# Two residual layers with a masked, per-batch weight on one core: the order of W's and y's work on VectorE and ScalarE

## The chip, the cores and the metric

The kernel runs on one core of a Trainium2 chip. The metric is the time of one execution on the device in microseconds (us), lower is better. The core's engines work side by side, each through its own list of instructions in order, and wait for each other by semaphores: TensorE (PE; PEld is its weight load) multiplies matrices, VectorE (DVE) and ScalarE (ACT) work elementwise, GpSimd (POOL) does little here, and SyncE (SP) issues the DMA transfers.

## The reference

```python
def L0(x, W, b, coeff, mask):
    output = jnp.einsum('bsi,oi->bso', x, W) + b
    sign = (2 * mask - 1).astype(x.dtype)
    diff = jnp.einsum('bsi,bio->bso', x, sign)
    return output + diff * coeff[:, None, None]

def L1(x, adapter_ids, base_weight, base_bias, lora_A_w, lora_B_w):
    result = jnp.einsum('bsd,od->bso', x, base_weight) + base_bias
    A = lora_A_w[adapter_ids]
    Bw = lora_B_w[adapter_ids]
    h = jnp.einsum('bsd,brd->bsr', x, A)
    return result + jnp.einsum('bsr,bor->bso', h, Bw)

x = x + L0(x, L0_cond_W, L0_cond_b, condB_coeff, mask)      # y
x = x + L1(x, ids, base_weight, base_bias, lora_A, lora_B)  # z, the output
```

x is 8 batches x 256 rows x 1024 columns in float32, the mask 8 x 1024 x 1024 in int32, both weights 1024 x 1024. Layer 1's weight is another one in each batch: W + coeff x (2 mask - 1), plus the identity for the residual. Layer 2's weight is the same for all batches, with a low-rank term of rank 16 that goes by the batch's adapter.

## The kernel before

**Parts.** Full float32 accuracy is had from matmuls of a rounded type. Each operand is split in a high part (rounded, ScalarE) and a low part (the rest, VectorE), and three products are summed: high x high, high x low and low x high. So whi and wlo are the parts of W, xhl holds both parts of x, yhl both of y, and w1hi and w1lo those of layer 2's weight.

**Steps.** A step n (0 to 63) is one block of 128 columns of y in one batch: b = n // 8, c = n % 8. TensorE does layer 1 of block n (`layer1(n)`, 16 matmuls, L756 and L758), waits for y's low part of block n-1 (`y_lo`), and then adds block n-1 to the batch's z (`layer2(n - 1, ...)`, 18 matmuls, L800 to L802). z of a batch stands in six PSUM banks until the batch is complete.

- W for a step: `load_mask` brings a block of the mask (512 KB) to one of four slots of wm; `make_w` (VectorE, L589) makes coefficient x mask + W in place; `chunk_hi` (ScalarE, L421) writes the high part, `chunk_lo` (VectorE, L596) the low part. It is made two steps ahead: step n makes W for n + 2.
- y of a step: when layer 1 is complete, `half_y` (ScalarE, L447) takes one half of the bank with the bias to ysum, `make_y` (VectorE, L603) adds the other half, `y_parts_hi` (ScalarE, L454) and `y_parts_lo` (VectorE, L607) write the parts to yhl. Both ysum and yhl have two slots.
- x of the next batch: `turn_rows` (VectorE transpose, L566) in steps c = 3 and 5, `rows_hi` (ScalarE, L432) in the same steps, `rows_lo` (VectorE, L572) in steps c = 4 and 6. The transpose waits for x's four DMAs.
- At a batch's first step (c = 0) TensorE does half of layer 1, then with y's last block the part of layer 2 that holds h, then the other half, and turns h (`turn_h`, L811). ScalarE moves h (`move_h`, L469) and writes its high part (`h_parts_hi`, L476 and L478), VectorE the low part (`h_parts_lo`, L617). Then TensorE ends z with `finish` (L829), and ScalarE and VectorE move three pieces of z each to zst (`move_z`, L489 and L629). TensorE's next layer 2 waits for these moves.

**Order.** The order of each engine's work is written out by hand in loops over n. No scheduler changes it. SyncE's list is in order too. At step n of it stands `load_mask(n + 4)`, which waits for the low part of W of step n; at c = 0 the six stores of z and the six DMAs of bt (`load_bt`) follow, and at c = 1, behind the mask, x of the next batch (`load_x`).

```python
for n in range(NS):
    b, c = divmod(n, KT)
    if n + 4 < NS:
        load_mask(n + 4)
    ...
    if c == 0 and b > 0:
        for q in range(4 if b == 1 else 6):
            store_z(b - 1, q)
        load_bt(b)
    if c == 1 and 0 < b < NB - 1:
        load_x(b + 1)
```

Of the kernel before, what the change touches and what calls it, by code (L numbers as in the profile page):

```python
# [16 lines left out]
def two_layer_kernel(nc, x, coeff, ids, mask, W0, b0, W1, b1, lora_a, lora_b, out):  # L17
    NB, S, D = x.shape
    NL, R, _ = lora_a.shape
    KT = D // P  # L20
    TG = HALF // P
    ST = S // P
    NS = NB * KT
# [37 lines left out]
    def x_split(b, g):  # L61

        return 4 + 2 * (b - 1) + 2 - g
# [5 lines left out]
    def l1_bank(n):  # L69
        if n < KT:  # L70
            return TB[0] if n == 0 else L1B
        return L1B + n % 2
# [12 lines left out]
    def sums_before(b):  # L85

        return 4 + 6 * (b - 1) if b else 0
# [9 lines left out]
    def h_hi_before(b):  # L97
        return 3 + 2 * (b - 1) if b else 0

    with ExitStack() as ctx:  # L100
# [297 lines left out]
        def _(act):  # L398
# [15 lines left out]
            def chunk_hi(n):  # L414
                act.wait_ge(w_made, n + 1)
                if n == 0:
                    act.wait_ge(coeff_made, 2)
                if n >= WS:
                    act.wait_ge(l1_done, n - WS + 1)
                b = n // KT  # L420
                nc.scalar.activation(whi[:, n % WS, :, :], wm[:, n % MS, :].rearrange("p (k o) -> p k o", k=KT),  # L421
                                     ACT.Identity, bias=cs_minus[:, b:b + 1]).then_inc(w_hi, 1)
# [18 lines left out]
            def half_y(n):  # L441
                act.wait_ge(l1_done, n + 1)
                if n == 0:
                    act.wait_ge(b0_moved, 1)
                if n >= 2:
                    act.wait_ge(y_lo, n - 1)
                nc.scalar.activation(ysum[:, n % 2, :], ps[:, l1_bank(n), S:2 * S], ACT.Identity,  # L447
                                     bias=b0col[:, n % KT:n % KT + 1]).then_inc(y_half, 1)

            def y_parts_hi(n):  # L450
                act.wait_ge(y_made, n + 1)
                if n >= 2:
                    act.wait_ge(l2_done, n - 1)
                nc.scalar.activation(yhl[:, n % 2, 0:S], ysum[:, n % 2, :], ACT.Copy).then_inc(y_hi, 1)  # L454

            def first_h_parts_hi():
                act.wait_ge(h_done, 1)
                act.wait_ge(consts_set, 2)
                nc.scalar.activation(ht[0:2 * R, :], ps[0:2 * R, HB, 0:S], ACT.Copy).then_inc(h_hi, 1)
                nc.scalar.activation(ht[64:64 + R, :], ps[0:R, HB, S:2 * S], ACT.Copy).then_inc(h_hi, 1)  # L460
                act.wait_ge(h_hi, 1)
                nc.scalar.activation(ht[96:96 + R, :], ht[0:R, :].bitcast(F32), ACT.Copy).then_inc(h_hi, 1)

            def move_h(b):
                act.wait_ge(h_done, b + 1)
                if b >= 2:
                    act.wait_ge(h_turned, b - 1)
                cut = z_cut(b, 0)[3]
                nc.scalar.activation(h_row[:, :, :], ps[:, ZB[0][0]:ZB[1][0] + 1, cut],  # L469
                                     ACT.Copy).then_inc(h_moved, 1)  # L470

            def h_parts_hi(b):
                act.wait_ge(h_turned, b)
                act.wait_ge(h_cleared, 1)
                act.wait_ge(z_done, sums_before(b))
                nc.scalar.activation(ht[0:R, :], ps[0:R, l1_bank(KT * b + 9), 0:S], ACT.Copy).then_inc(h_hi, 1)  # L476
                act.wait_ge(h_hi, h_hi_before(b) + 1)
                nc.scalar.activation(ht[96:96 + R, :], ht[0:R, :].bitcast(F32), ACT.Copy).then_inc(h_hi, 1)  # L478

            def first_move_z(st):  # L480
                act.wait_ge(z_done, 2 * st + 1)
                nc.scalar.activation(zst[:, st, 0:HALF], ps[:, Z0 + 2 * st, :], ACT.Copy).then_inc(z_moved_act, 1)

            def move_z(b, q):
                st, j = divmod(q, 3)
                act.wait_ge(z_done, sums_before(b) + q + 1)
                act.wait_ge(z_stored[st], 16 * stores_before(b))
                _, cut, cols, _ = z_cut(b, j)
                nc.scalar.activation(zst[:, st, cols], ps[:, ZB[st][j], cut], ACT.Copy).then_inc(z_moved_act, 1)  # L489
# [37 lines left out]
            for n in range(KT, NS):  # L527
                b, c = divmod(n, KT)
                if n == KT:
                    chunk_hi(n + 1)  # L530
                if c == 0 and b >= 2:
                    move_h(b - 1)
                    h_parts_hi(b - 1)
                half_y(n)
                if n == KT:
                    first_h_parts_hi()
                y_parts_hi(n)
                if n == KT:
                    chunk_hi(n + 2)
                    first_move_z(0)  # L540
                    first_move_z(1)
                elif c == 0:
                    for q in (0, 2, 4):
                        move_z(b - 1, q)
                if KT < n < NS - 2:
                    chunk_hi(n + 2)
                if c in (3, 5) and b + 1 < NB:
                    rows_hi(b + 1, 1 - (c - 3) // 2)
            move_h(NB - 1)
# [5 lines left out]
        def _(dve):  # L555
# [13 lines left out]
            def rows_lo(b, g):  # L569
                dve.wait_ge(x_hi, x_split(b, g))  # L570
                k = slice(g * TG, (g + 1) * TG)
                nc.vector.tensor_tensor(xhl[:, b % 2, k, S:2 * S], xt[:, :, :], xhl[:, b % 2, k, 0:S].bitcast(F32),  # L572
                                        ALU.subtract).then_inc(x_lo, 1)
# [9 lines left out]
            def make_w(n):  # L583
                b, c = divmod(n, KT)
                dve.wait_ge(mask_in[n % MS], 16 * (n // MS + 1))
                if b == 0:
                    dve.wait_ge(w0_copied, 2 * (c + 1))
                chunk = wm[:, n % MS, :]
                nc.vector.scalar_tensor_tensor(chunk, chunk.bitcast(I32), cs_twice[:, b:b + 1], w0t[:, c, :, :].rearrange("p k o -> p (k o)"),  # L589
                                               ALU.mult, ALU.add).then_inc(w_made, 1)  # L590

            def chunk_lo(n):
                dve.wait_ge(w_hi, n + 1)
                s = n % WS
                b = n // KT
                nc.vector.scalar_tensor_tensor(wlo[:, s, :, :], wm[:, n % MS, :].rearrange("p (k o) -> p k o", k=KT),  # L596
                                               cs_minus[:, b:b + 1], whi[:, s, :, :].bitcast(F32),
                                               ALU.add, ALU.subtract).then_inc(w_lo, 1)

            def make_y(n):  # L600
                dve.wait_ge(y_half, n + 1)
                row = ysum[:, n % 2, :]
                nc.vector.tensor_tensor(row, ps[:, l1_bank(n), 0:S], row, ALU.add).then_inc(y_made, 1)  # L603
# [6 lines left out]
            def first_h_parts_lo():  # L610
                dve.wait_ge(h_hi, 2)
                nc.vector.tensor_tensor(ht[32:32 + 2 * R, :], ps[0:2 * R, HB, 0:S], ht[0:2 * R, :].bitcast(F32),
                                        ALU.subtract).then_inc(h_lo, 1)

            def h_parts_lo(b):
                dve.wait_ge(h_hi, h_hi_before(b) + 1)
                nc.vector.tensor_tensor(ht[32:32 + R, :], ps[0:R, l1_bank(KT * b + 9), 0:S], ht[0:R, :].bitcast(F32),  # L617
                                        ALU.subtract).then_inc(h_lo, 1)
# [55 lines left out]
            for n in range(KT, NS):  # L674
                b, c = divmod(n, KT)
                if n == KT:
                    chunk_lo(n + 1)
                if c == 0 and b >= 2:
                    h_parts_lo(b - 1)
                make_y(n)  # L680
                if n == KT:
                    first_h_parts_lo()
                if n + 2 < NS:
                    make_w(n + 2)
                y_parts_lo(n)
                if c in (3, 5) and b + 1 < NB:
                    turn_rows(b + 1, 1 - (c - 3) // 2)
                if c in (4, 6) and b + 1 < NB:
                    rows_lo(b + 1, 1 - (c - 4) // 2)
                if n == KT:  # L690
                    first_move_z(0)
                    first_move_z(1)
                elif c == 0:
                    for q in (1, 3, 5):
                        move_z(b - 1, q)
                if n + 2 < NS:
                    chunk_lo(n + 2)
            h_parts_lo(NB - 1)
            for q in (1, 3, 5):
# [242 lines left out]
```

## Time and profile before

| | |
|---|---|
| time, median of 3 runs | 411.49 us (410.44 to 413.1) |
| the profiled execution's own time | 411.09 us |
| its span, first to last instruction | 409.3 us |
| mean granted TensorE clock | 1.00 of full speed |
| TensorE busy | 396.6 us (97%) |
| VectorE busy | 283.1 us (69%) |
| ScalarE busy | 183.8 us (45%) |

The rows further down have start times in us from the start of that span. A timeline row gives the start, the duration, the engine, the line of the program, the operation, and what is written from what. In square brackets stands how long the engine stood idle ahead of it, and what ended that idle time.

### The profile page before, as it was taken

The page shows a single profiled execution, that of the slowest core. Times are in us where ns is not written, and L with a number is a line of the kernel's source. Part 1 is how long each engine was busy: PE and PEld are TensorE (multiplying, and loading weights), DVE is VectorE, ACT ScalarE, POOL GpSimd, SP SyncE. Part 2 cuts the span into 40 slices and gives each one's busy share as a digit, 9 for nine tenths or more (in the row PEclk, how much of TensorE's full clock was granted, in tenths as well). Part 3 has the DMA queues.
Part 4 walks back from the last instruction along what each step waited for, and adds up shares of the span by engine and source line. Part 5 has one row for each costly group of instructions (what it writes and reads, how often), then busy time and mean ns, then how long its engine had stood idle before and what let it go on. Part 6 is the DMA issues. An engine that isn't in the chain of part 4 may idle for free.

```text
span 409.3 us, 6109 instructions
## 1 busy us (share of the span) xinstructions
PE 396.6 (97%) x2358; PEld 364.1 (89%) x2358; DVE 283.1 (69%) x343; ACT 183.8 (45%) x294; POOL 27.4 (7%) x42
## 2 busy tenths in 40 slices
PE   4899999999999999999999999999999999999995
PEld 3787788899999999999999999999999999999994
DVE  1667978867876688577886679575986679575622
ACT  3565675543444344344444345353444334353322
POOL 2224121000001000010001000010001000000000
PEclk9999999999999999999999999999999999999999
DMA  8999986259531893159531893249731793246002
GB/s 282 267 284 270 272 220 172 73 151 254 150 102 57 200 246 98 58 141 246 166 103 56 200 217 110 75 129 216 200 98 49 197 232 107 88 130 168 0 2 103
DMA packets 93633, 63.33 MB, mean 155 GB/s; under 512 B 3612, under 2 KB 90916, under 8 KB 93605
## 3 DMA queue, kind: packets, MB, share of 16 engines
q1 hardware_dynamic: 93586, 62.95, 58.3%
q8 instruction: 19, 0.31, 0.3%
q14 instruction: 10, 0.07, 0.1%
q10 hardware_dynamic: 18, 0.00, 0.0%
HBM read 51.39 MB, written 8.39 MB: 146 GB/s over the span
## 4 chain that ended last, share of the span: by engine, by line
PE 95%; DMA 2%; SPq 1%; DVE 1%; issue 0%; POOL 0%; ACT 0%; DVEq 0%
PE ps L756 29%; PE ps L758 15%; PE ps L802 13%; PE ps L801 13%; PE ps L800 13%; PE ps L734 4%; DMA w0raw<-in_L_cond_W_dram 2%; PE ps L780 2%; PE ps L778 2%; PE ps L779 2%; PE ps L829 2%; PE ps L766 1%; PE ps L811 0%; DVE wm L589 0%; POOL w0raw L341 0%
## 5 line engine op out<-in xcount | busy, mean ns | idle before, releaser
L756 PE MATMUL ps<-xhl,whi 128*128 128x512 f32 x512 | 184.8, 399 | 0.0
L758 PE MATMUL ps<-xhl,wlo 128*128 128x256 f32 x512 | 143.4, 280 | 0.0
L756 PEld LDWEIGHTS ps<-xhl,whi 128*128 128x128 f32 x512 | 96.5, 188 | 20.0 <-DVE xhl L579 0.4
L800 PE MATMUL ps<-w1hi,yhl 128*128 128x344 f32 (+1 forms) x336 | 108.1, 322 | 0.0
L802 PE MATMUL ps<-w1hi,yhl 128*128 128x344 f32 (+1 forms) x336 | 107.7, 321 | 0.0
L801 PE MATMUL ps<-w1lo,yhl 128*128 128x344 f32 (+1 forms) x336 | 107.6, 320 | 0.0
L596 DVE SCALAR_TENSOR_TENSOR wlo<-wm,cs_minus,whi 128x1024 fp32r<-128x1024 f32 x64 | 81.6, 1274 | 25.3 <-ACT whi L421 25.2
L758 PEld LDWEIGHTS ps<-xhl,wlo 128*128 128x128 f32 x512 | 97.0, 189 | 0.3
L421 ACT ACTIVATE whi<-wm,cs_minus 128x1024 fp32r<-128x1024 f32 x64 | 73.7, 1152 | 43.0 <-DVE wm L589 42.9
L589 DVE SCALAR_TENSOR_TENSOR wm<-wm,cs_twice,w0t 128x1024 f32<-128x1024 int32 x64 | 83.8, 1310 | 10.3 <-ACT w0t L402 8.4
L447 ACT ACTIVATE ysum<-ps,b0col 128x256 f32<-128x256 f32 x64 | 30.3, 474 | 85.5 <-PE ps L758 85.3
L800 PEld LDWEIGHTS ps<-w1hi,yhl 128*128 128x128 f32 x336 | 63.1, 188 | 2.6
L603 DVE TENSOR_TENSOR ysum<-ps,ysum 128x256 f32<-128x256 f32 x64 | 27.1, 424 | 53.1 <-ACT ysum L447 53.1
L801 PEld LDWEIGHTS ps<-w1lo,yhl 128*128 128x128 f32 x336 | 63.2, 188 | 0.0
L802 PEld LDWEIGHTS ps<-w1hi,yhl 128*128 128x128 f32 x336 | 63.1, 188 | 0.0
L454 ACT ACTIVATE yhl<-ysum 128x256 fp32r<-128x256 f32 x64 | 26.7, 417 | 28.6 <-DVE ysum L603 27.5
L566 DVE STREAM_TRANSPOSE xt<-xraw 128x1024 f32<-128x1024 f32 x14 | 31.1, 2220 | 4.2 <-DMA xraw<-in_x_dram 4.2
L607 DVE TENSOR_TENSOR yhl<-ysum,yhl 128x256 fp32r<-128x256 f32 x64 | 27.5, 430 | 1.5 <-ACT yhl L454 1.5
L432 ACT ACTIVATE xhl<-xt 128x1024 fp32r<-128x1024 f32 x14 | 14.9, 1061 | 20.5 <-DVE xt L566 20.5
L356 POOL CAST w1hi<-at 128x128 fp32r<-128x128 f32 x7 | 6.6, 940 | 223.7 <-PE ps L802 223.7
L572 DVE TENSOR_TENSOR xhl<-xt,xhl 128x1024 fp32r<-128x1024 f32 x14 | 17.1, 1221 | 0.2 <-ACT xhl L432 0.2
L734 PE MATMUL ps<-ident,w0raw 128*128 128x128 f32 x64 | 11.3, 313 | 5.7 <-POOL w0raw L341 5.7
(68 smaller groups left out, 217.3 us busy)
## 6 DMA issues: line engine op xcount, KB each, us to landing
wm<-in_mask_Bx4096x_ik_dram SPq DMA_DIRECT2D x64, 512.0 KB, 4.4
xraw<-in_x_dram SPq DMA_DIRECT2D x28, 256.0 KB, 5.8
w0raw<-in_L_cond_W_dram SPq DMA_DIRECT2D x8, 512.0 KB, 7.2
w1raw<-_L_cond_base_weight_dram SPq DMA_DIRECT2D x8, 512.0 KB, 7.4
out_dram<-zst SPq DMA_DIRECT2D x20, 172.0 KB, 2.1
bt<-bhl SPq DMA_DIRECT2D x48, 64.0 KB, 2.3
out_dram<-zst SPq DMA_DIRECT2D x8, 176.0 KB, 2.2
out_dram<-zst SPq DMA_DIRECT2D x8, 164.0 KB, 2.2
```

The source lines that it names most:

```text
L421: nc.scalar.activation(whi[:, n % WS, :, :], wm[:, n % MS, :].rearrange("p (k o) -> p k o", k=KT), ACT.Identity, bias=cs_minus[:, b:b + 1] ...
L447: nc.scalar.activation(ysum[:, n % 2, :], ps[:, l1_bank(n), S:2 * S], ACT.Identity, bias=b0col[:, n % KT:n % KT + 1]).then_inc(y_half, 1)
L566: nc.vector.transpose(xt[:, :, :].rearrange("p t (n q) -> p n t q", q=Q), xraw[:, :, :].rearrange("p n (i k) -> p n k i", k=KT)[:, :, g * ...
L589: nc.vector.scalar_tensor_tensor(chunk, chunk.bitcast(I32), cs_twice[:, b:b + 1], w0t[:, c, :, :].rearrange("p k o -> p (k o)"), ALU.mult, ...
L596: nc.vector.scalar_tensor_tensor(wlo[:, s, :, :], wm[:, n % MS, :].rearrange("p (k o) -> p k o", k=KT), cs_minus[:, b:b + 1], whi[:, s, :, ...
L607: nc.vector.tensor_tensor(yhl[:, n % 2, S:2 * S], ysum[:, n % 2, :], yhl[:, n % 2, 0:S].bitcast(F32), ALU.subtract).then_inc(y_lo, 1)
L734: op = nc.tensor.transpose(ps[:, bank, m * P:(m + 1) * P], cut[m], ident[:, :])
L756: nc.tensor.matmul(ps[:, bank, :], whi[:, s, k, :], xhl[:, b % 2, k, :], start=(k == 0), stop=False, skip_group_check=True)
L758: op = nc.tensor.matmul(ps[:, bank, 0:S], wlo[:, s, k, :], xhl[:, b % 2, k, 0:S], start=False, stop=(k == KT - 1), skip_group_check=True)
L800: nc.tensor.matmul(dst, hi, w1hi[:, c, cols], start=(c == 0), stop=False, skip_group_check=True)
L801: nc.tensor.matmul(dst, hi, w1lo[:, c, cols], start=False, stop=False, skip_group_check=True)
L802: op = nc.tensor.matmul(dst, lo, w1hi[:, c, cols], start=False, stop=(c == KT - 1), skip_group_check=True)
```

## The change

In the loop over steps 8 to 63, from step 9 on, VectorE's and ScalarE's work for W of step n + 2 is put ahead of the work for y of step n. Before, VectorE's order was sum of y, product of W, low part of y, transpose or low part of x, moves of z, low part of W. Now it is product of W, low part of x, low part of W, sum of y, low part of y, transpose of x, moves of z. ScalarE's high part of W goes from the end of the step to ahead of the half of y. Step 8 and the steps of batch 0 keep their order. No instruction is added or taken away, and TensorE's, GpSimd's and SyncE's lists stay as they are.

```diff
@@ -531,6 +531,8 @@
                 if c == 0 and b >= 2:
                     move_h(b - 1)
                     h_parts_hi(b - 1)
+                if KT < n < NS - 2:
+                    chunk_hi(n + 2)
                 half_y(n)
                 if n == KT:
                     first_h_parts_hi()
@@ -542,8 +544,6 @@
                 elif c == 0:
                     for q in (0, 2, 4):
                         move_z(b - 1, q)
-                if KT < n < NS - 2:
-                    chunk_hi(n + 2)
                 if c in (3, 5) and b + 1 < NB:
                     rows_hi(b + 1, 1 - (c - 3) // 2)
             move_h(NB - 1)
@@ -677,23 +677,26 @@
                     chunk_lo(n + 1)
                 if c == 0 and b >= 2:
                     h_parts_lo(b - 1)
+                if KT < n < NS - 2:
+                    make_w(n + 2)
+                if c in (4, 6) and b + 1 < NB:
+                    rows_lo(b + 1, 1 - (c - 4) // 2)
+                if KT < n < NS - 2:
+                    chunk_lo(n + 2)
                 make_y(n)
                 if n == KT:
                     first_h_parts_lo()
-                if n + 2 < NS:
                     make_w(n + 2)
                 y_parts_lo(n)
                 if c in (3, 5) and b + 1 < NB:
                     turn_rows(b + 1, 1 - (c - 3) // 2)
-                if c in (4, 6) and b + 1 < NB:
-                    rows_lo(b + 1, 1 - (c - 4) // 2)
                 if n == KT:
                     first_move_z(0)
                     first_move_z(1)
                 elif c == 0:
                     for q in (1, 3, 5):
                         move_z(b - 1, q)
-                if n + 2 < NS:
+                if n == KT:
                     chunk_lo(n + 2)
             h_parts_lo(NB - 1)
             for q in (1, 3, 5):
```

VectorE at a batch's first step (c = 0), before. In brackets stand the semaphores that an instruction waits for: h_hi and y_hi are ScalarE's high parts, y_half its half of y, w_hi its high part of W, mask_in a mask's landing.

```order
L617 TENSOR_TENSOR ht<-ps,ht 16x256 [waits h_hi]
L603 TENSOR_TENSOR ysum<-ps,ysum 128x256 [waits y_half]
L589 SCALAR_TENSOR_TENSOR wm<-wm,cs_twice,w0t 128x1024 [waits mask_in2]
L607 TENSOR_TENSOR yhl<-ysum,yhl 128x256 [waits y_hi]
L629 COPY zst<-ps 128x344 [waits z_stored0,z_done]
L629 COPY zst<-ps 128x336 [waits z_stored1,z_done]
L629 COPY zst<-ps 128x344 [waits z_stored1,z_done]
L596 SCALAR_TENSOR_TENSOR wlo<-wm,cs_minus,whi 128x1024 [waits w_hi]
```

The same step of VectorE in the changed kernel:

```order
L617 TENSOR_TENSOR ht<-ps,ht 16x256 [waits h_hi]
L589 SCALAR_TENSOR_TENSOR wm<-wm,cs_twice,w0t 128x1024 [waits mask_in2]
L596 SCALAR_TENSOR_TENSOR wlo<-wm,cs_minus,whi 128x1024 [waits w_hi]
L603 TENSOR_TENSOR ysum<-ps,ysum 128x256 [waits y_half]
L607 TENSOR_TENSOR yhl<-ysum,yhl 128x256 [waits y_hi]
L629 COPY zst<-ps 128x344 [waits z_stored0,z_done]
L629 COPY zst<-ps 128x336 [waits z_stored1,z_done]
L629 COPY zst<-ps 128x344 [waits z_stored1,z_done]
```

The sum of y (L603) and with it the moves of z (L629) now stand behind both of VectorE's instructions for W.

ScalarE at the same step, before. l1_done is TensorE's end of a layer 1, l2_done that of a layer 2, w_made VectorE's product.

```order
L469 ACTIVATE h_row<-ps 128x32 [waits h_turned,h_done]
L476 ACTIVATE ht<-ps 16x256 [waits z_done,h_cleared,h_turned]
L478 ACTIVATE ht<-ht 16x256 [waits h_hi]
L447 ACTIVATE ysum<-ps,b0col 128x256 [waits y_lo,l1_done]
L454 ACTIVATE yhl<-ysum 128x256 [waits l2_done,y_made]
L489 ACTIVATE zst<-ps 128x328 [waits z_stored0,z_done]
L489 ACTIVATE zst<-ps 128x352 [waits z_stored0,z_done]
L489 ACTIVATE zst<-ps 128x344 [waits z_stored1,z_done]
L421 ACTIVATE whi<-wm,cs_minus 128x1024 [waits l1_done,w_made]
```

The same step of ScalarE in the changed kernel:

```order
L469 ACTIVATE h_row<-ps 128x32 [waits h_turned,h_done]
L476 ACTIVATE ht<-ps 16x256 [waits z_done,h_cleared,h_turned]
L478 ACTIVATE ht<-ht 16x256 [waits h_hi]
L421 ACTIVATE whi<-wm,cs_minus 128x1024 [waits l1_done,w_made]
L447 ACTIVATE ysum<-ps,b0col 128x256 [waits y_lo,l1_done]
L454 ACTIVATE yhl<-ysum 128x256 [waits l2_done,y_made]
L489 ACTIVATE zst<-ps 128x328 [waits z_stored0,z_done]
L489 ACTIVATE zst<-ps 128x352 [waits z_stored0,z_done]
L489 ACTIVATE zst<-ps 128x344 [waits z_stored1,z_done]
```

The high part of W (L421) has gone from behind the moves of z to ahead of the half of y (L447).

## Rows read from the trace of the kernel before

**Rows 1.** The page's busy time: us, share of the span, instructions.

```profile
PE 396.6 (97%) x2358; PEld 364.1 (89%) x2358; DVE 283.1 (69%) x343; ACT 183.8 (45%) x294; POOL 27.4 (7%) x42
```

**Rows 2.** The page's chain of waits that ended last, by engine.

```profile
PE 95%; DMA 2%; SPq 1%; DVE 1%; issue 0%; POOL 0%; ACT 0%; DVEq 0%
```

**Rows 3.** Timeline of TensorE, first matmuls of layer 2 in steps 32 to 34.

```profile
216.48 0.32 PE L800 MATMUL ps<-w1hi,yhl 128*128 128x344 f32 x1
...
224.71 0.33 PE L800 MATMUL ps<-w1hi,yhl 128*128 128x352 f32 x1
...
230.37 0.32 PE L800 MATMUL ps<-w1hi,yhl 128*128 128x352 f32 x1
```

**Rows 4.** Waits between 120 and 400 us: total us, times, longest.

```profile
DVE ysum L603 <- ACT ysum L447: 46.8, 49, 4.3
```

**Rows 5.** Timeline of VectorE in steps 31 and 32.

```profile
213.29 1.28 DVE L589 SCALAR_TENSOR_TENSOR wm<-wm,cs_twice,w0t 128x1024 f32<-128x1024 int32 x1
214.48 0.42 DVE L607 TENSOR_TENSOR yhl<-ysum,yhl 128x256 fp32r<-128x256 f32 x1
215.78 1.28 DVE L596 SCALAR_TENSOR_TENSOR wlo<-wm,cs_minus,whi 128x1024 fp32r<-128x1024 f32 x1 [0.88 <-ACT whi L421]
219.66 0.41 DVE L617 TENSOR_TENSOR ht<-ps,ht 16x256 fp32r<-16x256 f32 x1 [2.60 <-ACT ht L476]
220.61 0.42 DVE L603 TENSOR_TENSOR ysum<-ps,ysum 128x256 f32<-128x256 f32 x1 [0.54 <-ACT ysum L447]
...
222.58 1.34 DVE L629 COPY zst<-ps 128x344 f32<-128x344 f32 x3
```

**Rows 6.** Timeline of ScalarE in steps 31, 32 and 35.

```profile
214.60 1.15 ACT L421 ACTIVATE whi<-wm,cs_minus 128x1024 fp32r<-128x1024 f32 x1 [0.77 <-DVE wm L589]
...
221.07 0.42 ACT L454 ACTIVATE yhl<-ysum 128x256 fp32r<-128x256 f32 x1 [0.49 <-DVE ysum L603]
...
242.09 1.07 ACT L432 ACTIVATE xhl<-xt 128x1024 fp32r<-128x1024 f32 x1 [2.60 <-DVE xt L566]
```

**Rows 7.** Timeline of VectorE, low part of h in batches 2 and 6.

```profile
127.07 0.41 DVE L617 TENSOR_TENSOR ht<-ps,ht 16x256 fp32r<-16x256 f32 x1 [2.60 <-ACT ht L476]
...
312.27 0.41 DVE L617 TENSOR_TENSOR ht<-ps,ht 16x256 fp32r<-16x256 f32 x1 [2.60 <-ACT ht L476]
```

**Rows 8.** Timeline of VectorE, x's first transposes in batches 2 to 6; one low part.

```profile
146.44 2.22 DVE L566 STREAM_TRANSPOSE xt<-xraw 128x1024 f32<-128x1024 f32 x1 [0.40 <-DMA xraw<-in_x_dram]
...
192.32 2.25 DVE L566 STREAM_TRANSPOSE xt<-xraw 128x1024 f32<-128x1024 f32 x1
...
239.88 2.18 DVE L566 STREAM_TRANSPOSE xt<-xraw 128x1024 f32<-128x1024 f32 x1 [1.23 <-DMA xraw<-in_x_dram]
...
245.42 1.22 DVE L572 TENSOR_TENSOR xhl<-xt,xhl 128x1024 fp32r<-128x1024 f32 x1
...
285.83 2.21 DVE L566 STREAM_TRANSPOSE xt<-xraw 128x1024 f32<-128x1024 f32 x1 [0.85 <-DMA xraw<-in_x_dram]
...
332.48 2.18 DVE L566 STREAM_TRANSPOSE xt<-xraw 128x1024 f32<-128x1024 f32 x1 [1.23 <-DMA xraw<-in_x_dram]
```

**Rows 9.** Timeline of TensorE in the first layer 1.

```profile
16.00 0.63 PE L756 MATMUL ps<-xhl,whi 128*128 128x512 f32 x1
...
16.64 0.58 PE L756 MATMUL ps<-xhl,whi 128*128 128x512 f32 x1
...
17.74 0.50 PE L756 MATMUL ps<-xhl,whi 128*128 128x512 f32 x1
18.08 0.28 PE L758 MATMUL ps<-xhl,wlo 128*128 128x256 f32 x1
18.20 0.40 PE L756 MATMUL ps<-xhl,whi 128*128 128x512 f32 x1
```

**Rows 10.** Timeline of the SyncE queue, batch 3's z and the next mask.

```profile
221.85 3.60 SPq L286 DMA_DIRECT2D out_dram<-zst  x6
...
229.30 0.60 SPq L224 DMA_DIRECT2D wm<-in_mask_Bx4096x_ik_dram  x1
```

**Rows 11.** The page's DMA issues: KB each, median us from issue to landing.

```profile
wm<-in_mask_Bx4096x_ik_dram SPq DMA_DIRECT2D x64, 512.0 KB, 4.4
```

## The prediction

> **What bounds the kernel now.** I read the page's busy shares first, then its chain of waits, then the timelines of TensorE, VectorE and ScalarE around one batch boundary. TensorE is busy 97% of the span and VectorE 69% [rows 1]; the chain that ends last lies on TensorE for 95% [rows 2]. Past start-up TensorE hardly waits. One step of it, layer 1 of output block n and then layer 2 of block n-1, takes 230.37 - 224.71 = 5.66 us [rows 3]. So nothing that VectorE or ScalarE do faster can shorten the middle of the span, and the question is only whether the new order makes them late.
>
> They are not busy all the time because they wait: between 120 and 400 us VectorE stands 46.8 us in 49 waits for ScalarE's half of y [rows 4], which itself waits for the end of layer 1. The change puts W's work for step n+2 into that gap. Whether it fits is a matter of one serial chain, not of busy shares.
>
> **The new chain of one step.** The order of work of the new kernel is, on VectorE: product (L589), low part (L596), sum of y (L603), low part of y (L607). On ScalarE: high part of W (L421), half of y (L447), high part of y (L454). Each of the six other than the half of y now waits for the one before it on the other engine, since VectorE's low part of W follows ScalarE's high part, and the sum of y is queued behind that low part. Durations: product 1.28, low part of W 1.28, sum of y 0.42, low part of y 0.42 [rows 5]; high part of W 1.15, high part of y 0.42 [rows 6]. A hand-over between the two engines costs 0.03 to 0.04 (product ends 214.57, high part starts 214.60; that ends 215.75, low part starts 215.78; sum ends 221.03, high part of y starts 221.07) and the next instruction on the same engine starts about 0.08 before the end of the one ahead (214.48 against 214.57) [rows 5, 6]. So from a product to the next product:
> 1.28 + 0.03 + 1.15 + 0.03 + 1.28 - 0.08 + 0.42 + 0.04 + 0.42 + 0.04 + 0.42 - 0.08 = 4.95 us.
> That is less than 5.66, so a step without other work is made up with 0.7 us to spare. In the old order the product lay beside ScalarE's high part of y and ScalarE's high part of W beside VectorE's other work, which is why the old order had more room at equal busy time.
>
> **The rest of a batch.** Eight steps of TensorE take 46.30 us ((312.27 - 127.07) / 4, the low part of h in batches 2 and 6 [rows 7]). I follow batch 4 from that low part at 219.66 [rows 5], since VectorE waits there for TensorE in either order: it starts free of what went before.
> - low part of h: 0.41 - 0.08 = 0.33
> - eight chains, for y of blocks 32 to 39: 8 x 4.95 = 39.6
> - three moves of z, after y of block 32: 1.34 - 0.08 = 1.26 [rows 5]
> - two transposes of x, after y of 35 and of 37: 2.18 - 0.08 and 2.23 - 0.08, about 4.25 (2.18 to 2.25 long [rows 8])
> - x's high parts on ScalarE (1.07 [rows 6]) lie beside VectorE's product of 1.28, and x's low parts (1.22 [rows 8]) beside ScalarE's high part of W with its two hand-overs, 1.15 + 0.03 + 0.03 = 1.21: nothing; at worst 0.1 each
> - the overlap at the end, since the last value must be complete: 0.08
> The sum is 45.5 us to the end of the low part of y of block 39. TensorE wants that value in the middle of layer 1 of block 40, and starts 0.04 later with some 0.10 for the restart (the first matmul after a wait at the start of the kernel took 0.50, a usual one 0.40 [rows 9]). From there to the next low part of h are 219.66 - 216.48 = 3.18 us [rows 3, 5]. Batch: 45.5 + 0.14 + 3.18 = 48.8 us against 46.30, so **2.5 us more in each batch** without any wait for data. The steps on the way: y of block 32 ends 5.4 us after 219.66, at 225.0, and TensorE wants it at 224.71 [rows 3]; y of 33 ends 231.2 against 230.37, so the first waits come at once.
>
> **Wait for x.** The move of z now comes behind W's work. ScalarE's high part of y of block 32 started at 221.07; now it starts at 219.66 + 0.33 + 1.28 + 0.03 + 1.15 + 0.03 + 1.28 - 0.08 + 0.42 + 0.04 = 224.14, 3.07 later. The SyncE queue is in order: the stores of z wait for these moves (221.85 [rows 10]), behind them stand bt's rows, then a mask (229.30) and then x of the next batch. All of it shifts by 3.07. The transpose of x waited for x already in four of batches 2 to 6 (those at 146.44, 239.88, 285.83 and 332.48; the one at 192.32 just did not) [rows 8]. New landing: old + 3.07. VectorE is free for it 0.33 + 4 x 4.95 + 1.26 = 21.4 us after the low part of h, in batch 4 at 241.05; x is there at 242.95. Waits by batch, with the low parts of h 46.30 apart: 1.0, 0.6, 1.9, 1.5, 1.8, together 6.8 us. These go straight into the chain. The mask ahead of x is wanted at 236.1 and lands at 229.30 + 3.07 + 4.4 = 236.8 [rows 10, 11]; what VectorE loses there it would have waited for x anyway.
>
> **The ends.** Batch 7 loads no x; its second y comes 0.33 + 4.95 + 1.26 + 4.95 + 0.08 + 0.14 = 11.7 us after the low part of h, TensorE wants it after 230.37 - 219.66 = 10.7: 1.0 us, and nothing after that. Batch 1 keeps the old order at its first step and waits for no moves: between 0 and 2.5 - 1.26 = 1.2; I take 0.7. The last two steps have no W in either order.
>
> **Sum.** 5 x 2.5 + 6.8 + 1.0 + 0.7 = 21.0 us. The profiled execution took 411.09 with a span of 409.3, which lies 0.4 below the median of 411.49; so 430.3 for the new span, 432.1 for such an execution and 432.5 against the median. The product, made 4.7 us earlier relative to layer 1, gains nothing: no wait of TensorE for W is in the middle of the span to be removed.
>
> **Rivals.** (1) *No loss.* The chains would have to overlap more than I believe: TensorE's waits vanish if a chain takes 4.95 - 2.5/8 = 4.6 us and x lands as before. Every term has a row, so only the shift of x can be softer. If x lands early enough for all batches, 21.0 - 6.8 = 14.2 are left: 425.7. For no measurable change both must hold; that would give 411 to 415. Chance 0.06. (2) *Faster.* A W that is ready a step earlier would take away waits of TensorE for W's low part and let the mask's slot come free sooner. For it speaks that 46.8 us of VectorE's idle time is filled. Against it: TensorE is covered to 95% by its own work [rows 2]; the mechanism decides only if those gaps of TensorE that the rows do not show are waits for W. All that is outside TensorE in the chain is 5% and start-up has nearly all of it; a hundredth of the span, 4 to 5 us, is the most: 407. Chance 0.02. (3) *The clock.* The granted clock is at its full level over the whole span on the page, and a matmul after TensorE's wait at 17.74 took 0.50; the two before it began 0.64 apart with 0.63 and 0.58 for one, against 0.40 later [rows 9], which could be a lower clock that the page does not show. The new kernel makes four or five waits per batch, one of up to 2 us. If after the longest in each batch one step ran at 1.2 GHz in place of 2.4, it would take some 5.66 us more, of which 0.7 is room: 5 x 5 = 25 on top, 457. The start speaks for it only after much longer gaps. Chance 0.05.
> The Trainium skill ("TensorE: Matmul & The Clock Gate", section "A second HAM failure mode: psum-queue depth-cycling") says that short, frequent idle spells between groups of matmuls can make the clock swing between its two levels. By that rule rival 3 would hold; the trace before has no such spells past start-up to test it.
> (4) *More wait for data.* x and three masks share the queue; every further us of x's landing costs 5 us. Part of the range.
>
> **Numbers.** Forecast 0.87, rivals 0.06, 0.02, 0.05. A chain is known to about 0.05 us, which is 40 x 0.05 = 2 us; x may land 1.5 us earlier or 1 us later than I have it, which is -6.1 (the five waits cut to 0, 0, 0.4, 0 and 0.3) to +5 us. That gives 424 to 440. Changes under 1% (4 us) are about what a measurement of this kernel cannot tell from none. Faster 0.02, same 0.06, slower 0.92.
>
> **What would show it.** The chain of waits goes from TensorE over to VectorE and ScalarE, with product, high part, low part, sum, high, low of y in turn. Low parts of h lie 49 to 51 us apart, not 46.3. TensorE's load at L800 waits for L607 four to five times per batch, longest for block 36. The transpose of x waits 1 to 2 us for its DMA. If TensorE's step stays at 5.66 everywhere and h keeps its spacing, the chain is wrong; if the spacing is 48.8, x is.

## The result and the profile after

The changed kernel takes 432.53 us (median of 4 runs, 430.74 to 433.2), the kernel before 412.1 us in the runs beside it. The ratio is 1.0499 with a 95% interval of 1.0459 to 1.0538: 5% slower. The profiled execution took 433.2 us, its span is 431.4 us against 409.3.

The page's busy time and its chain of waits, after:

```profile
PE 404.4 (94%) x2358; PEld 363.9 (84%) x2358; DVE 285.8 (66%) x343; ACT 179.5 (42%) x294; POOL 22.3 (5%) x42
PE 36%; DVE 31%; ACT 13%; SPq 8%; DMA 7%; issue 3%; POOL 1%; DVEq 0%
```

VectorE and ScalarE are busy for nearly as many us as before (285.8 against 283.1, 179.5 against 183.8 [rows 1]) and for a smaller share of the span. What changed is the chain: TensorE holds 36% of it, not 95% [rows 2]. VectorE and ScalarE are far from full, yet the kernel is slower, and the chain names who sets the pace.

The waits between 120 and 420 us (total, times, longest), after:

```profile
ACT whi L421 <- DVE wm L589: 69.0, 37, 4.1
ACT yhl L454 <- DVE ysum L603: 62.6, 48, 1.3
DVE wlo L596 <- ACT whi L421: 45.1, 37, 1.2
DVE yhl L607 <- ACT yhl L454: 23.2, 48, 0.5
PE ps L803 <- DVE yhl L607: 13.5, 28, 1.2
DVE wm L589 <- DMA wm<-in_mask_Bx4096x_ik_dram: 6.7, 4, 2.3
DVE ysum L603 <- ACT ysum L447: 3.6, 1, 3.6
```

The wait that the change wanted to fill, VectorE's for the half of y, is gone but for the last two steps, which have no W (46.8 us before [rows 4]; the one of 3.6 us here and one of 4.3 us at 420.30). In its place VectorE and ScalarE wait for each other, and TensorE has a new wait: 28 times at the first matmul of layer 2 (L803 here) for y's low part. It waits nowhere else in this stretch. The 13.5 us are only its idle time; what a wait costs beyond that stands further down.

VectorE's timeline in batch 4 after, which answers to [rows 5]:

```profile
227.99 0.41 DVE L617 TENSOR_TENSOR ht<-ps,ht 16x256 fp32r<-16x256 f32 x1 [3.35 <-ACT ht L476]
228.43 1.28 DVE L589 SCALAR_TENSOR_TENSOR wm<-wm,cs_twice,w0t 128x1024 f32<-128x1024 int32 x1
230.94 1.28 DVE L596 SCALAR_TENSOR_TENSOR wlo<-wm,cs_minus,whi 128x1024 fp32r<-128x1024 f32 x1 [1.22 <-ACT whi L421]
232.14 0.41 DVE L603 TENSOR_TENSOR ysum<-ps,ysum 128x256 f32<-128x256 f32 x1
233.04 0.43 DVE L607 TENSOR_TENSOR yhl<-ysum,yhl 128x256 fp32r<-128x256 f32 x1 [0.48 <-ACT yhl L454]
233.38 1.35 DVE L629 COPY zst<-ps 128x344 f32<-128x344 f32 x3
234.64 1.28 DVE L589 SCALAR_TENSOR_TENSOR wm<-wm,cs_twice,w0t 128x1024 f32<-128x1024 int32 x1
...
239.59 1.28 DVE L589 SCALAR_TENSOR_TENSOR wm<-wm,cs_twice,w0t 128x1024 f32<-128x1024 int32 x1
...
246.91 1.28 DVE L589 SCALAR_TENSOR_TENSOR wm<-wm,cs_twice,w0t 128x1024 f32<-128x1024 int32 x1 [2.30 <-DMA wm<-in_mask_Bx4096x_ik_dram]
...
251.86 2.19 DVE L566 STREAM_TRANSPOSE xt<-xraw 128x1024 f32<-128x1024 f32 x1
...
279.25 0.41 DVE L617 TENSOR_TENSOR ht<-ps,ht 16x256 fp32r<-16x256 f32 x1 [3.35 <-ACT ht L476]
```

Up to 239.59 each row waits for ScalarE or follows at once: the serial chain. From product to product (234.64 to 239.59) it is 4.95 us. The batch is 279.25 - 227.99 = 51.26 us long, against 46.3 [rows 7]. In it lies one wait for data, 2.30 us, and it is for the mask. The transpose of x shows no wait, unlike [rows 8].

The SyncE queue in that batch, after, against [rows 10]:

```profile
233.36 2.91 SPq L286 DMA_DIRECT2D out_dram<-zst  x6
236.31 3.13 SPq L276 DMA_DIRECT2D bt<-bhl  x5
239.49 0.59 SPq L277 DMA_DIRECT2D bt<-bhl  x1
240.12 0.60 SPq L224 DMA_DIRECT2D wm<-in_mask_Bx4096x_ik_dram  x1
```

The first store begins 233.36 - 227.99 = 5.4 us after the low part of h (2.2 before), the mask is issued 12.1 us after it (9.6 before) and lands 6.8 us later, at 246.91. VectorE was ready for it at 244.6.

TensorE around the wait of that step:

```profile
250.95 0.28 PE L761 MATMUL ps<-xhl,wlo 128*128 128x256 f32 x1
252.00 0.43 PE L803 MATMUL ps<-w1hi,yhl 128*128 128x352 f32 x1 [0.77 <-DVE yhl L607]
252.26 0.32 PE L804 MATMUL ps<-w1lo,yhl 128*128 128x352 f32 x1
```

The first matmul after a wait takes 0.43 and the next one 0.32, as in a stretch without waits. But the wait costs more than its 0.77 us of idle time. From the last matmul of layer 1 to the second of layer 2 are 252.26 - 250.95 = 1.31 us here and 224.87 - 224.59 = 0.28 before, as the timeline of the kernel before shows:

```profile
224.59 0.28 PE L758 MATMUL ps<-xhl,wlo 128*128 128x256 f32 x1
224.71 0.33 PE L800 MATMUL ps<-w1hi,yhl 128*128 128x352 f32 x1
224.87 0.32 PE L801 MATMUL ps<-w1lo,yhl 128*128 128x352 f32 x1
```

That is 1.03 us later, 0.26 more than the idle time. In a dense stretch the matmuls overlap in the trace (each starts before the end of the one ahead), so part of the loss counts as busy: TensorE is busy 404.4 us in place of 396.6 for the same 2358 matmuls. The 28 waits by this reading cost 13.5 + 28 x 0.26 = 20.8 us, an estimate from this wait (two others of the batch, at 233.52 and 259.01, have 0.27 for the 0.26), near the 22.1 us that the span grew.

### The profile page after: what moved, and what is told of

Same layout as the page of the kernel before. It is cut to its first block, busy times and chain, and to the rows that moved or that the text cites. A ratio compares the mean times of both kernels' runs of the same rounds, so it can differ in the third digit from the quotient of the medians.

```text
span 431.4 us, 6109 instructions
## 1 busy us (share of the span) xinstructions
PE 404.4 (94%) x2358; PEld 363.9 (84%) x2358; DVE 285.8 (66%) x343; ACT 179.5 (42%) x294; POOL 22.3 (5%) x42
## 4 chain that ended last, share of the span: by engine, by line
PE 36%; DVE 31%; ACT 13%; SPq 8%; DMA 7%; issue 3%; POOL 1%; DVEq 0%
PE ps L759 10%; DVE wlo L596 10%; DVE wm L589 10%; ACT whi L421 9%; DVE xt L566 5%; PE ps L761 5%; PE ps L803 4%; PE ps L737 4%; DMA wm<-in_mask_Bx4096x_ik_dram 4%; PE ps L805 4%; PE ps L804 4%; ACT yhl L454 3%; SPq L276 3%; DVE ysum L603 3%; SPq L286 2%
## 5 line engine op out<-in xcount | busy, mean ns | idle before, releaser
L803 PE MATMUL ps<-w1hi,yhl 128*128 128x344 f32 (+1 forms) x336 | 111.3, 331 | 13.5 <-DVE yhl L607 13.5
L421 ACT ACTIVATE whi<-wm,cs_minus 128x1024 fp32r<-128x1024 f32 x64 | 73.7, 1151 | 82.8 <-DVE wm L589 81.3
L805 PE MATMUL ps<-w1hi,yhl 128*128 128x344 f32 (+1 forms) x336 | 107.7, 321 | 0.0
L589 DVE SCALAR_TENSOR_TENSOR wm<-wm,cs_twice,w0t 128x1024 f32<-128x1024 int32 x64 | 83.1, 1299 | 16.4 <-ACT w0t L402 8.7
L803 PEld LDWEIGHTS ps<-w1hi,yhl 128*128 128x128 f32 x336 | 63.1, 188 | 24.2 <-DVE yhl L607 22.9
L447 ACT ACTIVATE ysum<-ps,b0col 128x256 f32<-128x256 f32 x64 | 29.3, 458 | 16.1 <-PE ps L761 16.1
L603 DVE TENSOR_TENSOR ysum<-ps,ysum 128x256 f32<-128x256 f32 x64 | 26.7, 418 | 8.3 <-ACT ysum L447 8.3
L617 DVE TENSOR_TENSOR ht<-ps,ht 16x256 fp32r<-16x256 f32 x7 | 2.9, 414 | 23.6 <-ACT ht L476 23.6
```

What stands on the lines that cost most here:

```text
L803: nc.tensor.matmul(dst, hi, w1hi[:, c, cols], start=(c == 0), stop=False, skip_group_check=True)
L805: op = nc.tensor.matmul(dst, lo, w1hi[:, c, cols], start=False, stop=(c == KT - 1), skip_group_check=True)
```

## The experiments

In what follows a *chain* is one step's serial chain, from one product of W to the next. The theory: from batch 1 on, the length of a batch is the serial sum of VectorE's and ScalarE's hand-overs, 8 chains with z's moves and x's transposes, plus what VectorE waits for data that the late moves of z push back. TensorE only follows. The rivals: a *fixed lateness* (each us of W's work ahead of y costs in proportion), and *the queue* (all of the loss comes from z's late moves and what stands behind the stores). All times are medians, all ratios are to the kernel before (411.7 to 411.9 us beside these runs). Where two altered kernels are compared, the difference of their medians is given; taken from the ratios it comes out 1 to 2.5 us smaller or larger, so it is no closer than that.

**One part alone: the product first.** Of the kernel before, in VectorE's list:

```diff
+                if KT < n < NS - 2:
+                    make_w(n + 2)
                 make_y(n)
                 if n == KT:
                     first_h_parts_lo()
-                if n + 2 < NS:
                     make_w(n + 2)
```

> The kernel before with one part of the change alone: VectorE's product of W goes ahead of the sum of y; both parts of W stay behind y. Theory of the serial chain (the batch's length is the sum of the hand-overs between VectorE and ScalarE): the product lies beside ScalarE's half of y, and behind it come sum, high part of y, then ScalarE's high part of W and VectorE's low part: 1.20 + 0.42 + 0.04 + 0.42 - 0.10 + 1.15 + 0.03 + 1.20 = 4.36 us per step, well below the 5.66 of TensorE; a batch by that chain is 44.4 us, under 46.3. So 412, as the kernel before, within 1%. Rival of a fixed lateness (any W work ahead of y keeps TensorE waiting in proportion to its time): the product is 1.28 of the 3.7 us put ahead of y, a third of the 20 us, so 419. Rival of the queue (all comes from z's moves being late): they are late by about 0.7 of 3.1 us, 416.

Measured: 411.88 us, ratio 1.0008 (0.9986 to 1.003). No loss, as the chain says, and fixed lateness and queue are both out at their numbers: z's first store was late as the queue rival has it (in batch 4 it began 2.9 us after the low part of h in place of 2.2), and nothing was lost by it. The waits of this run (120 to 420 us) show a second thing:

```profile
DVE xt L566 <- DMA xraw<-in_x_dram: 9.8, 5, 2.9
DVE wm L589 <- DMA wm<-in_mask_Bx4096x_ik_dram: 3.5, 4, 1.3
```

VectorE waits here for 13.3 us for data, twice as long as in the changed kernel, and it costs nothing, since VectorE has room in the old order of the parts. The same kind of wait costs its full length where VectorE's chain sets the pace.

**Half undone: the low part of W behind y.** Of the changed kernel, in VectorE's list:

```diff
                     rows_lo(b + 1, 1 - (c - 4) // 2)
-                if KT < n < NS - 2:
-                    chunk_lo(n + 2)
                 make_y(n)
...
-                if n == KT:
+                if n + 2 < NS:
                     chunk_lo(n + 2)
```

> The changed kernel with VectorE's low part of W put back behind y; product and ScalarE's high part of W stay ahead. Serial chain: ScalarE's half of y is now queued behind the high part and nothing of VectorE lies beside it: 1.28 + 0.03 + 1.15 - 0.10 + 0.46 + 0.04 + 0.42 + 0.04 + 0.42 + 0.04 + 0.42 - 0.08 + 1.28 - 0.08 = 5.32 us per step in place of 4.95. Seven of them and the 4.20 of the last up to the low part of y make the batch 1.8 us longer than in the changed kernel without waits for data; the mask is wanted 1.1 later and comes 0.8 earlier, so most of its wait (1.35 on average) goes. Together 0.7 us more per batch: 434 to 438, slower than the changed kernel although y comes earlier in each step's list. Rival of fixed lateness: y has 2.4 in place of 3.7 us ahead of it: about 425. Rival of the queue: z's moves are late by 2.2 in place of 3.1: about 426.

Measured: 437.56 us, ratio 1.0652 (1.062 to 1.0684). Slower than the changed kernel although less stands ahead of y. This is where the theories differ most, and only the serial chain has the sign and the size. VectorE's timeline in this run:

```profile
242.57 1.28 DVE L589 SCALAR_TENSOR_TENSOR wm<-wm,cs_twice,w0t 128x1024 f32<-128x1024 int32 x1
245.43 0.42 DVE L603 TENSOR_TENSOR ysum<-ps,ysum 128x256 f32<-128x256 f32 x1 [1.58 <-ACT ysum L447]
246.34 0.42 DVE L607 TENSOR_TENSOR yhl<-ysum,yhl 128x256 fp32r<-128x256 f32 x1 [0.48 <-ACT yhl L454]
246.68 1.28 DVE L596 SCALAR_TENSOR_TENSOR wlo<-wm,cs_minus,whi 128x1024 fp32r<-128x1024 f32 x1
247.88 1.28 DVE L589 SCALAR_TENSOR_TENSOR wm<-wm,cs_twice,w0t 128x1024 f32<-128x1024 int32 x1
```

The chain is 247.88 - 242.57 = 5.31 us (5.32 expected): VectorE stands 1.58 us while ScalarE does the high part of W and then the half of y. TensorE waits in this run for W's low part too, but only once at a matmul, 0.4 us; by the waits that is no second cause of this size.

**The old order at the batch's first step.** In the changed kernel both engines do step c = 0 as before:

```diff
-                if KT < n < NS - 2:
+                if KT < n < NS - 2 and c > 0:
                     chunk_hi(n + 2)
...
-                if KT < n < NS - 2:
+                if KT < n < NS - 2 and c > 0:
                     make_w(n + 2)
...
-                if KT < n < NS - 2:
+                if KT < n < NS - 2 and c > 0:
                     chunk_lo(n + 2)
                 make_y(n)
                 if n == KT:
                     first_h_parts_lo()
+                if c == 0:
                     make_w(n + 2)
```

and the high and the low part of W behind z's moves at c = 0.

> The changed kernel with the old order in each batch's first step (c = 0) alone, on both engines. Serial chain: y of that step is out after 2.9 us and z is moved as early as before, so the mask and x are issued as in the kernel before; from the low part of h to the next step's product 5.4 us in place of 6.65. Then seven chains of 4.95: 5.38 + 34.65 + 0.08 + 4.25 + 0.14 + 3.18 = 47.7 us a batch against 46.3, next to no wait for the mask. 5 x 1.4 + 0.7 in batch 1, nothing in batch 7: 8 us over the kernel before, 420. Queue rival: all gone, 412. Fixed lateness: seven of eight steps are left, 429.

Measured: 419.46 us, ratio 1.0203 (1.0159 to 1.0248). ScalarE's first high part of h in batches 2 and 7 of this run:

```profile
128.72 0.38 ACT L476 ACTIVATE ht<-ps 16x256 fp32r<-16x256 f32 x1 [1.43 <-PE ps L816]
...
367.22 0.38 ACT L476 ACTIVATE ht<-ps 16x256 fp32r<-16x256 f32 x1 [1.43 <-PE ps L816]
```

(367.22 - 128.72) / 5 = 47.70 us a batch, the expected 47.7. One step of eight done in the old order takes away 13 of 20 us (12 by the ratios): the chain loses 1.3 us there and the mask comes in time (0.3 us of waits for it are left).

**The mask and x ahead of the stores.** SyncE's list of the changed kernel:

```diff
-                if n + 4 < NS:
+                if n + 4 < NS and not (c == 1 and b > 0):
                     load_mask(n + 4)
...
                 if c == 0 and b > 0:
+                    load_mask(n + 5)
+                    if b < NB - 1:
+                        load_x(b + 1)
                     for q in range(4 if b == 1 else 6):
                         store_z(b - 1, q)
                     load_bt(b)
-                if c == 1 and 0 < b < NB - 1:
-                    load_x(b + 1)
```

> The changed kernel with SyncE's list altered: at a batch's first step the next mask and x's four loads are issued ahead of the stores of z and bt's rows. Nothing else. Serial chain: the waits of VectorE for the mask (2.0, 0, 2.3, 1.2, 1.2 in the changed kernel's trace) go, low parts of h lie 48.9 to 49.1 us apart in each batch, 5 x 2.7 + 1.0 + 0.8 = 15 us over the kernel before: 426 to 427. Queue rival: 412, since mask and x are early now. Fixed lateness: 427 too.

Measured: 426.7 us, ratio 1.0402 (1.0354 to 1.0449). No wait of VectorE for DMA is left between 120 and 420 us. The page's chain of waits of this run:

```profile
DVE 39%; PE 36%; ACT 16%; DMA 4%; issue 2%; SPq 1%; POOL 0%; DVEq 0%
```

VectorE has more of the chain than TensorE. ScalarE's timeline, first high part of h in batches 2 and 7:

```profile
126.47 0.38 ACT L477 ACTIVATE ht<-ps 16x256 fp32r<-16x256 f32 x1 [1.43 <-PE ps L815]
...
371.06 0.38 ACT L477 ACTIVATE ht<-ps 16x256 fp32r<-16x256 f32 x1 [1.43 <-PE ps L815]
```

A batch is (371.06 - 126.47) / 5 = 48.92 us. By the medians 5.8 of the 20.4 us lost are waits for data that the queue held back; by the ratios 4.0, by the length of the five batches in the two traces 7.1 (251.7 against 244.6 us). So 4 to 7 us go with early data, and 13 to 16 us stay.

**A shorter chain.** The run before, with half of each product left out from step 11 on, so that the output is not the reference's:

```diff
+                h = slice(0, D // 2 if n > KT + 2 else D)
-                nc.vector.scalar_tensor_tensor(chunk, chunk.bitcast(I32), cs_twice[:, b:b + 1], w0t[:, c, :, :].rearrange("p k o -> p (k o)"),
+                nc.vector.scalar_tensor_tensor(chunk[:, h], chunk[:, h].bitcast(I32), cs_twice[:, b:b + 1],
+                                               w0t[:, c, :, :].rearrange("p k o -> p (k o)")[:, h],
                                                ALU.mult, ALU.add).then_inc(w_made, 1)
```

> The run with the hoisted mask and x, and the product of W made over only 512 of its 1024 columns from step 11 on (the other half of W stays the bare mask in its raw form: part of the computation is left out). The order of work is the changed kernel's. Serial chain: the product takes about 0.7 in place of 1.28, a chain 4.37, a batch 48.9 - 8 x 0.58 = 44.3 us, less than TensorE's 46.3: TensorE binds again, 412 to 414. Fixed lateness: y is still 3.1 of 3.7 us late, 412 + 15 x 3.1 / 3.7 = 425.

Measured: 412.11 us, ratio 0.999 (0.9963 to 1.0016). All of the loss is gone with the order of the changed kernel kept. The groups by line and shape of this run show the product's length (busy us, mean ns). Below it stands the page's chain of waits:

```profile
L591 DVE SCALAR_TENSOR_TENSOR wm<-wm,cs_twice,w0t 128x512 f32<-128x512 int32 x53 | 39.1, 738 | 0.2
```

```profile
PE 90%; DMA 5%; SPq 2%; POOL 1%; issue 1%; DVE 0%; DVEq 0%
```

0.54 us less per chain, 4.3 per batch: by the sum 48.9 - 4.3 = 44.6, under TensorE's 46.3, and TensorE has the chain again.

**A longer chain, in both orders.** One more instruction between the parts of y:

```diff
             def y_parts_lo(n):
                 dve.wait_ge(y_hi, n + 1)
+                if n > KT:
+                    nc.vector.tensor_tensor(scratch[:, :], ysum[:, n % 2, :], yhl[:, n % 2, 0:S].bitcast(F32),
+                                            ALU.subtract)
```

> The changed kernel with one more VectorE instruction of 128x256 between the high and the low part of y in each step from 9 on (it writes to a scratch tile). Serial chain: each chain is 0.34 to 0.42 longer, so a batch 8 x 0.36 = 2.9 longer, less what the wait for the mask gives back (wanted 3 x 0.36 = 1.1 later, and z and so the mask 0.0 later for ScalarE's moves): some +1.9 x 5 + 2.5 in batch 1 + 0.7: 444 to 447. Were TensorE still what binds, the instruction would cost nothing: 432.

> The kernel before with the same additional VectorE instruction. Serial chain: in the old order the chain has more than 0.4 us of room per step, so it costs nothing: 412, within 0.5%.

Measured: 446.01 us in the changed kernel (1.0797, 1.0748 to 1.0846), 412.22 us in the kernel before (1.0001, 0.998 to 1.0023). The same instruction costs 13.5 us in one order (12 by the ratios) and nothing that can be measured in the other. In VectorE's timeline of the first run the chain is 247.55 - 242.27 = 5.28 us, 0.33 more than 4.95, with the extra instruction in it:

```profile
242.27 1.27 DVE L590 SCALAR_TENSOR_TENSOR wm<-wm,cs_twice,w0t 128x1024 f32<-128x1024 int32 x1
...
246.87 0.42 DVE L609 TENSOR_TENSOR scratch<-ysum,yhl 128x256 f32<-128x256 f32 x1 [0.48 <-ACT yhl L455]
247.22 0.42 DVE L611 TENSOR_TENSOR yhl<-ysum,yhl 128x256 fp32r<-128x256 f32 x1
247.55 1.28 DVE L590 SCALAR_TENSOR_TENSOR wm<-wm,cs_twice,w0t 128x1024 f32<-128x1024 int32 x1
```

**The new order in three steps of eight.** On both engines `early` says whether W's work goes ahead of y; where it is false the old order stands. Of the kernel before, in VectorE's list:

```diff
+                early = KT < n < NS - 2 and c in (1, 2, 7)
+                if early:
+                    make_w(n + 2)
+                    chunk_lo(n + 2)
                 make_y(n)
...
-                if n + 2 < NS:
+                if n + 2 < NS and not early:
                     make_w(n + 2)
...
-                if n + 2 < NS:
+                if n + 2 < NS and not early:
                     chunk_lo(n + 2)
```

> The new order in steps c = 1, 2 and 7 of each batch alone, the old order in the other five (c = 0 with the moves of z, c = 3 to 6 with x). Serial chain: 4.95 us is less than TensorE's 5.66, and the steps with additional work are in the old order that has room for it, so TensorE never waits: 412 to 413. Fixed lateness: three eighths of the changed kernel's loss, 419 to 420.

Measured: 413.08 us, ratio 1.0029 (1.0 to 1.0059). A step by itself fits in the new order, as 4.95 against 5.66 says. Some 0.3% may be a real cost: TensorE's weight loads still wait for y six times in this run, 0.3 us at the longest, and a batch is 46.52 us long in its trace (low parts of h from 127.14 to 359.73, five batches) against 46.31 in the trace before (127.07 to 358.62), 1 us in all. What these few waits come from was not followed further.

## Why the prediction was right

432.5 us was forecast, 432.53 measured, the range was 424 to 440. That the two numbers meet is luck: the four runs lie between 430.74 and 433.2, and the loss was forecast as 21.0 us and measured as 20.4 by the medians and 22.1 in the span of the profiled execution (430.3 forecast, 431.4 measured). The mechanism is the one forecast, with one wait in the wrong place. Point by point:

- *TensorE binds, the new order can only make it late.* Right: its share of the chain fell from 95% to 36%, and no run was faster than the kernel before by more than the noise.
- *A chain of 4.95 us.* Right: 4.95 in the trace after, 5.31 where one place in it was altered (5.32 expected).
- *2.5 us more per batch without waits for data.* Right, a little small: with all data early a batch is 48.92 us, 2.6 over 46.3; in the changed kernel it is 48.9 to 49.1 after its waits for data are taken off. The low part of h costs the chain 0.44 (227.99 to 228.43), not 0.33, since the product behind it does not start before its end.
- *6.8 us of waits for data.* The sum was right: 6.7 in the trace, 4 to 7 by the run that takes them away. **The place was wrong.** The step on the wait for x had VectorE wait for x in each of batches 2 to 6, and dismissed the mask in front of it with "what VectorE loses there it would have waited for x anyway". The trace shows the waits at the product, for the mask (four of them, 2.3 us at the longest), and none at the transpose: by the time that VectorE had the mask, made W and gone through y, x had landed (in batches 2 and 3 within 0.1 us of it). The mask took the room that I gave to x. I had one row for it, of batch 4. In batches 2 to 6 of the changed kernel it was issued 13.9, 12.1, 12.1, 13.4 and 13.2 us after the low part of h (12.7 expected) and landed 4.7, 4.5, 6.8, 4.5 and 4.6 us later (4.4 expected), while VectorE wanted it after 16.6 us (16.4 expected). That makes the waits of 2.0, 0.1, 2.3, 1.2 and 1.2 us. So in batches 2, 5 and 6 the late issue made most of the wait, and only in batch 4 the long landing. The spread of the issue was there to be seen in the kernel before, where it came 10.1, 9.6, 9.6, 10.6 and 10.4 us after the low part of h. Why the landing in batch 4 took longer is open. The two waits, for the mask and for x, stand in one chain, so the larger would cover the other; that the sum came out near is luck beyond that: single batches were 51.05, 49.07, 51.26, 50.21 and 50.12 us, against 49.8, 49.4, 50.7, 50.3 and 50.6 by my terms.
- *The ends.* Batch 7 is 1.2 us longer (45.56 against 44.39; 1.0 forecast). In batch 1 the forecast 0.7 was too much. The low part of h of batch 2 comes 0.8 us later (127.87 in place of 127.07 [rows 7]), but 0.6 of that was there at step 8, ahead of all that the change touches. VectorE's timeline at the first low part of h, in the kernel before:

```profile
80.61 0.41 DVE L612 TENSOR_TENSOR ht<-ps,ht 32x256 fp32r<-32x256 f32 x1
```

and in the changed kernel:

```profile
81.24 0.41 DVE L612 TENSOR_TENSOR ht<-ps,ht 32x256 fp32r<-32x256 f32 x1
```

  Batch 1 itself grew from 46.46 to 46.63 us, by 0.2. The start-up before it varies from trace to trace (80.3 to 83.2 us in the runs here).
- *Longest wait of TensorE for block 36.* Right: in batch 4 after, it is 1.13 us at the matmul, in the step of the first transpose; the one for block 35, with the mask in it, is 0.77. There were five or six waits per batch at the weight load (two in batch 7), four or five forecast. The restart cost the 0.10 us that the forecast took for it (0.43 - 0.32 at the first matmul).
- *The clock.* No sign of it: the granted clock is 1.00 of full speed, 2.4 GHz, in the stretches of 4 us from 228 to 260 us and over 92 to 431 us as a whole, and matmuls behind a wait are back at 0.32 us at once. The Trainium skill ("TensorE: Matmul & The Clock Gate", section "A second HAM failure mode: psum-queue depth-cycling") tells of a kernel in which frequent short idle spells between groups of matmuls make the clock swing; here 28 such spells of up to 1.2 us between 120 and 420 us did not.

The rivals fell by experiment: no loss needs a chain of 4.6 us or less with early data, which the half product provides (4.95 - 0.54 = 4.4, and the loss is gone) and the changed kernel does not (4.95); the queue alone is worth 4 to 7 of 20.4 us; a lateness in proportion fails for the product alone (nothing lost) and for the low part put back (more lost).

## What to carry to other kernels

Two engines that hand work to each other were limited here by the sum of their instructions and hand-overs in their lists' order, not by their busy shares: at 66% and 42% busy they set the pace in the new order, and at 69% and 45% they had at least a third of a us per step to spare in the old one. Before filling an engine's idle gap, write down the chain of one step in the new order, add what comes once per batch, and compare with the step and the batch of the engine that binds. In this kernel the order in which one engine works on W while the other is on y was worth more than the one that starts W as early as it can. And whatever stands behind the moved work in an in-order DMA queue comes later too: here a mask behind stores that waited for a later copy. Take such a landing from the rows of every batch and not from one: the issue of this mask spread over 1 us from batch to batch already in the kernel before.

## What the runs showed of the hardware

- A hand-over between VectorE and ScalarE cost 0.03 to 0.04 us, and the next instruction on the same engine began about 0.08 us before the end that the profile shows for the one ahead. With both, the sum for a chain was within 0.02 us of the trace (4.95 against 4.93 to 4.95, 5.32 against 5.31), and that for a batch of 49 us without waits within 0.2. One exception: the product behind the low part of h began 0.03 us after its end (227.99 + 0.41 to 228.43).
- The landing of a 512 KB mask, in the place behind z's stores and bt's rows, took 4.5 us in one batch of the changed kernel and 6.8 us in the next (4.5 to 4.7 in the other three). No other single step of the forecast was off by as much.
- A short wait cost TensorE 0.26 us beyond its idle time in the trace, 0.10 of it at the first matmul (0.43 in place of 0.32 us); the next ones took their usual time.
